# Attention and a ternary FFN on one core: first FFN weights made in two halves, query and key parts moved to GpSimd, and another written-out order

## The reference, cut to what matters

```python
xn = (x - mean) / sqrt(var + 1e-5)
# attention, 8 heads: queries and keys of 3 numbers a head, values of 16
scores = (q3 . k3) * scale + (q3 . dir_h) * (k3 . dir_h)     # causal
attn = softmax(scores) @ v ;  attn_out = attn @ Wo.T
# FFN, hidden size 512
def ternary(w): s = clip(mean(abs(w), axis=1), 1e-5); return clip(round(w / s), -1, 1), s
h = xn @ (t1 * s1).T + gate * (xn @ v.T @ fast_b.T @ u.T)
ffn_out = max(h, 0)**2 @ (t2 * s2).T
out = x + attn_out + ffn_out
```

## Time and profile before

| | before |
|---|---|
| median of 3 executions | 159.28 us (159.23 to 160.33) |
| profiled execution | 160.0 us, of which the span of its records is 158.3 us, and 1.7 us lie around it |
| granted clock of TensorE | 1.00 over the whole span |
| busy PE / DVE / ACT / POOL | 148.7 / 127.0 / 123.1 / 70.3 us |
| instructions | 3300 |
| zero matmuls | 47, the last at 52 us |

### The profile page before, as it was taken

How to read it: one execution, slowest core, us unless ns; L and a number is a source line. 1 busy time by engine, 2 the same in 40 slices (tenths; PEclk the granted TensorE clock), 3 DMA queues, 4 the chain that set the end, 5 groups by cost and what they waited for, 6 DMA issues and landing times.

```text
span 158.3 us, 3300 instructions
## 1 busy us (share of the span) xinstructions
PE 148.7 (94%) x1109; PEld 63.1 (40%) x1109; DVE 127.0 (80%) x423; ACT 123.1 (78%) x222; POOL 70.3 (44%) x126
## 2 busy tenths in 40 slices
PE   6999999999999999999999988898999989999992
PEld 2374446232242252232222222321736226885672
DVE  4688998999999999989999999999498885320442
ACT  0779795589588978898679999889899998878700
POOL 5038005942999689006931067013863225161520
PEclk9999999999999999999999999999999999999999
DMA  3760000240100170600000020000110200120202
GB/s 100 196 200 0 4 4 0 46 86 0 33 4 2 21 146 4 132 1 15 18 4 0 0 37 4 0 0 0 37 33 0 66 4 0 34 69 3 61 12 66
DMA packets 16621, 5.71 MB, mean 36 GB/s; under 512 B 11292, under 2 KB 16476, under 8 KB 16604
## 3 DMA queue, kind: packets, MB, share of 16 engines
q1 hardware_dynamic: 16208, 5.34, 14.8%
q10 hardware_dynamic: 396, 0.16, 0.4%
HBM read 1.96 MB, written 1.05 MB: 19 GB/s over the span
## 4 chain that ended last, share of the span: by engine, by line
PE 50%; ACT 32%; issue 7%; DVE 7%; POOL 1%; ACTq 1%; POOLq 0%; DVEq 0%
ACT Pr L757 21%; PE obank L973 8%; PE vbank L791 7%; PE vbank L922 6%; PE obank L798 6%; PE abank L950 5%; ACT abank L743 5%; PE abank L897 5%; PE abank L902 4%; DVE vbank L591 3%; PE abank L878 3%; ACT xn L663 2%; PE vbank L993 2%; DVE pm L588 2%; PE abank L849 1%
## 5 line engine op out<-in xcount | busy, mean ns | idle before, releaser
L757 ACT ACTIVATE Pr<-abank 128x1024 f32<-128x1024 f32 (+3 forms) x96 | 74.3, 817 | 7.9 <-PE abank L950 3.3
L591 DVE CUSTOM_DVE_ANT_0 vbank<-vbank,mask_row 128x128 f32<-128x128 f32 (+3 forms) x128 | 58.9, 524 | 4.4 <-PE vbank L922 3.9
L922 PE MATMUL vbank<-QK 32*128 32x512 bf16 (+3 forms) x192 | 40.4, 329 | 1.5 <-DVE xn L634 0.3
L588 DVE TENSOR_REDUCE pm<-vbank 128x1 f32<-128x512 f32 x64 | 39.5, 683 | 0.7 <-PE vbank L922 0.5
L973 PE MATMUL obank<-Pr,V 128*32 128x512 f32 (+3 forms) x384 | 39.2, 496 | 0.4 <-POOL Pr L454 0.4
L950 PE MATMUL abank<-QK 32*128 32x512 bf16 (+3 forms) x192 | 30.8, 331 | 2.1 <-ACT Pr L757 1.4
L454 POOL TENSOR_SCALAR_AFFINE_SELECT Pr<-Pr 128x512 f32<-128x512 f32 x32 | 20.1, 636 | 27.8 <-ACT Pr L757 27.6
L922 PEld LDWEIGHTS vbank<-QK 32*128 32x128 bf16 x192 | 11.5, 91 | 40.2 <-issue 17.4
L743 ACT ACTIVATE abank<-abank 128x256 f32<-128x256 f32 x64 | 23.3, 377 | 4.5 <-PE abank L950 3.7
L591 DVE DVE_READ_ACCUMULATOR2_ANT pm<- 128x1 f32 x128 | 18.4, 144 | 0.0
L798 PE MATMUL obank<-mask_row 128*128 128x512 bf16 x47 | 16.5, 447 | 1.3 <-POOL mask_row L386 1.3
(11 more groups left out here) (111 smaller groups left out, 129.5 us busy)
## 6 DMA issues: line engine op xcount, KB each, us to landing
x_sb<-in_L_attn_x SPq DMA_DIRECT2D x4, 256.0 KB, 3.5
out_y<-xn SPq DMA_DIRECT2D x8, 128.0 KB, 1.8
wfc_sb<-in_L_ffn_w_fc SPq DMA_DIRECT2D x1, 256.0 KB, 3.7
wpj_sb<-in_L_ffn_w_proj SPq DMA_DIRECT2D x1, 256.0 KB, 2.6
QK<-X SPq DMA_TRANSPOSE x10, 2.5
k_sb<-in_consts SPq DMA_DIRECT2D x1, 64.0 KB, 2.8
Wv_sb<-in_L_attn_Wv ACTq DMA_DIRECT2D x1, 64.0 KB, 3.4
Wo_sb<-in_L_attn_Wo ACTq DMA_DIRECT2D x1, 64.0 KB, 3.8
```

The lines of the kernel that those rows point to most:

```text
L588: last = nc.vector.tensor_reduce(out=least, in_=s_n, op=ALU.min, axis=AX.X)
L591: last = nc.vector.tensor_tensor_reduce(out=s_n, in0=s_n, in1=mask_row[:, CH - keys:CH], scale=1.0, scalar=3.0e38, op0=ALU.add, op1=ALU.mi ...
L757: nc.scalar.activation(Pr[:, n % PSLOTS, 2 * pair:2 * pair + 2, 0:cols], src[:, :, 0:cols], ACT.Exp, scale=-1.0).then_inc(free(unit), 1)
L922: last = nc.tensor.matmul(o[:, at:at + keys], QK[r, quarter(b, chunk), 0, g, q0:q0 + P], QK[r, quarter(b, half), 1, g, 0:keys], start=True ...
```

## The change

1. **First weights in halves.** "signs 0" makes four comparisons of 128x256 in place of two of 128x512 and counts each in `fc_signs`. "ternary 0" and the new "ternary 2" do half of the four GpSimd instructions each (128x256), counting `w1_ready` to 1 and 2. "w1" becomes "w1a" and "w1b", each with its low-rank product of 256 columns, two transposes, a bank of its own and its own copy by ACT. The first hidden-layer item of a quarter waits for w1a, the second for w1b.
2. **Query and key parts of quarters 1 to 3.** ACT now copies the numbers as float32 to SBUF instead of rounding them. GpSimd rounds, subtracts, rounds, subtracts (four instructions in place of two). DVE has no part in them, and ACT's copy of the values waits for no one.
3. **36 zero matmuls** in place of 47.
4. **Another order** of everything. In letters, the first hundred or so items:

```diff
@@ -126,7 +126,7 @@
-FILLERS = 47
+FILLERS = 36
...
@@ -150,7 +150,8 @@
         "W": [("mix", 0), ("weights", "wqk"), ("weights", "wvo")],
-        "F": [("signs", 0), ("ternary", 0)], "U": [("weights", k) for k in ("lora_u", "lora_b", "w1")],
+        "F": [("signs", 0), ("ternary", 0), ("ternary", 2)],
+        "U": [("weights", k) for k in ("lora_u", "lora_b", "w1a", "w1b")],
...
@@ -163,12 +164,12 @@
...
@@ -396,14 +397,20 @@
             wp = wpj_sb[:, :].rearrange("p (j c) -> p j c", j=HC)
-            ternaries = ((wfc_sb[:, :, :], fc_sc[:, 0, :, None].to_broadcast([P, HC, C]), fc_signs, w1_ready),
-                         (wp, pj_sc[:, 0:1, None].to_broadcast([P, HC, C]), pj_signs, w2_ready))
+            def hidden_half(n):
+                j = slice(n * HC // 2, (n + 1) * HC // 2)
+                return (wfc_sb[:, j, :], fc_sc[:, 0, j, None].to_broadcast([P, HC // 2, C]), tern[:, 0, :, j, :],
+                        fc_signs, 2 * (n + 1), w1_ready)
+            ternaries = (hidden_half(0), (wp, pj_sc[:, 0:1, None].to_broadcast([P, HC, C]), tern[:, 1, :, :, :],
+                                          pj_signs, 2, w2_ready), hidden_half(1))
...
                 if item[0] == "ternary":
-                    w, sc, signs, ready = ternaries[item[1]]
-                    pool.wait_ge(signs, 2)
-                    above, below = tern[:, item[1], 0, :, :], tern[:, item[1], 1, :, :]
+                    w, sc, marks, signs, count, ready = ternaries[item[1]]
+                    pool.wait_ge(signs, count)
+                    above, below = marks[:, 0, :, :], marks[:, 1, :, :]
...
@@ -411,7 +418,9 @@
                     q = item[1]
-                    pool.wait_ge(res_ready, q + 1)
+                    pool.wait_ge(hi_ready, q + 1)
+                    link(nc.gpsimd.tensor_copy(bf16_part(q, 0), rest(q)))
+                    link(nc.gpsimd.tensor_tensor(rest(q), rest(q), bf16_part(q, 0), ALU.subtract))
...
@@ -438,7 +447,7 @@
                     if c == 0:
-                        pool.wait_ge(w1_ready, 1)
+                        pool.wait_ge(w1_ready, 2)
...
@@ -535,14 +544,11 @@
                     nc.vector.tensor_copy(wall[:, C:VQK], filled(item)[:, 0:2 * NQ]).then_inc(free(item), 1)
-                elif kind == "qkv":
-                    q = item[1]
-                    src = qkv_view(item)[:, :, C:VQK].rearrange("p t (s c) -> p t s c", s=2 * G) if q else qk_rest()
-                    dve.wait_ge(hi_ready, q + 1)
-                    nc.vector.tensor_tensor(rest(q) if q else src, src, bf16_part(q, 0),
-                                            ALU.subtract).then_inc(res_ready, 1)
+                elif item == ("qkv", 0):
+                    dve.wait_ge(hi_ready, 1)
+                    nc.vector.tensor_tensor(qk_rest(), qk_rest(), bf16_part(0, 0), ALU.subtract).then_inc(res_ready, 1)
...
@@ -558,10 +564,12 @@
                         link(nc.vector.tensor_scalar(fc_sc[:, 2, :], fc_sc[:, 0, :], -0.5, None, ALU.mult))
-                        for k, op in enumerate((ALU.is_gt, ALU.is_lt)):
-                            nc.vector.tensor_tensor(tern[:, 0, k, :, :], wfc_sb[:, :, :],
-                                                    fc_sc[:, 1 + k, :, None].to_broadcast([P, HC, C]),
-                                                    op).then_inc(fc_signs, 1)
+                        for n in range(2):
+                            j = slice(n * HC // 2, (n + 1) * HC // 2)
+                            for k, op in enumerate((ALU.is_gt, ALU.is_lt)):
+                                nc.vector.tensor_tensor(tern[:, 0, k, j, :], wfc_sb[:, j, :],
+                                                        fc_sc[:, 1 + k, j, None].to_broadcast([P, HC // 2, C]),
+                                                        op).then_inc(fc_signs, 1)
...
@@ -692,7 +700,9 @@
                         src = qkv_view(item)[:, :, C:VQK].rearrange("p t (s c) -> p t s c", s=2 * G)
-                    nc.scalar.copy(bf16_part(q, 0), src).then_inc(hi_ready, 1)
+                    nc.scalar.copy(rest(q) if q else bf16_part(q, 0), src).then_inc(hi_ready, 1)
...
@@ -703,7 +713,6 @@
                     else:
-                        act.wait_ge(res_ready, q + 1)
...
@@ -766,8 +775,9 @@
                         ins = nc.scalar.activation(loraB, src[0:RANK, :], ACT.Copy, scale=gate_c[:, 0:1])
-                    elif item[1] == "w1":
-                        ins = nc.scalar.copy(w1T[:, :], src[:, :])
+                    elif item[1] in ("w1a", "w1b"):
+                        at = HID // 2 * (item[1] == "w1b")
+                        ins = nc.scalar.copy(w1T[:, at:at + HID // 2], src[:, 0:HID // 2])
...
@@ -820,14 +830,16 @@
                         last = nc.tensor.matmul(o[0:RANK, :], fb_sb[:, :], uT, start=True, stop=True)
-                    elif item[1] == "w1":
-                        pe.wait_ge(w1_ready, 1)
+                    elif item[1] in ("w1a", "w1b"):
+                        second = item[1] == "w1b"
+                        at = HID // 2 * second
+                        pe.wait_ge(w1_ready, 1 + second)
                         read(("weights", "lora_b"))
-                        nc.tensor.matmul(o[:, :], v_sb[:, :], loraB, start=True, stop=False)
-                        for j in range(HC):
-                            last = nc.tensor.matmul(o[:, j * P:(j + 1) * P], wfc_sb[:, j, :], ident,
-                                                    start=False, stop=j == HC - 1)
+                        nc.tensor.matmul(o[:, 0:HID // 2], v_sb[:, :], loraB[:, at:at + HID // 2], start=True, stop=False)
+                        for j in range(HC // 2):
+                            last = nc.tensor.matmul(o[:, j * P:(j + 1) * P], wfc_sb[:, HC // 2 * second + j, :], ident,
+                                                    start=False, stop=j == HC // 2 - 1)
...
@@ -892,7 +904,7 @@
                     o = empty(item)
-                    read(("weights", "w1"))
+                    read(("weights", "w1b" if j else "w1a"))
...
```

More of the change, by code:

```diff
@@ L165 @@
 WEAVE = """
-KKNNKKKKWKKKKKNKWNKCKXWFUQKKNKILVKNFUECKENNKKKKMMUNKMKNNMMHMMHMMXMJXQMMMVMQHMNILMVHRMMHMMHMMETKMMSIMAOMHMGMHMK
-MAMKMKMOAGOKDMGAMKMROKGKAMMHMOMMGHMMKXMAOMSJKMAGKKMTAOMKGKMDOALGMKMOAMKKGOKMGAMKKMKAODMGORKGMMDAPMAMOPMDSMGODA
-GOAOPPTPMMGGAQAMVMPDDMMAAMPMMAPMInAMPMAMPHAMHMJMMAAEMOOMMGLPMMGEAMMOAPMOGMARPMMGOAGADMOOPGGAMOMGTAMHMMSHMMDAnM
-PMAAMMPMADDMPAPPMMAMAPMASMAOMMnGOGPMMAOMRPGMAAOMMODTPGGAMOMMAPGAOGOMGMAAMMDPDMDAMAMPPMAMMASMPHAMHMMPAMMAMnPAMO
-MGPMOGMAPMMMADPYOGROGTSAOBAGOMAGOBGAYOMGAAMMDPMDMAPMADMPPABAMMMABAYASOMGAOMPMMAPGnOAMMPGMAROPGMMOMAGDAOPOYTDGP
-GAOAMMOGBMDADGPPOAGOBAGOBRTADGYBPnOGDAOAOGBYAGOAYOGBDBAGAOOPGPPABYGAOGDOAODGPPDGBYDAAPPOPOGGnDPPnBBYBYY
+KKKKKKNNKWNCKKKWKNFKKFKKXWUQKNIKKLKNNUEVUKNMNMHNMFMHUMMXEMMMQIMVNMLHMMMHMMXMHKRCHJMMMQMEMKVTMMAMOSMHGMMHMJKMMA
+RMOHGMAMNDOMHMMMKTGIJMAAOMMKOKMGKAGMMOLGKMAOKGXMDKMAOAMOGMKMAMGDOKDKMMAKMGKKMMAPOGMMROAGAOMPDMEOGGMAAOPOGMPMTM
+GPAQDDDVAMMnMPAMAMAMMIPAMMLAMPAMMAPMMHPMMOGAEOMHPMMGAPMOMAMMGODPAGMMOSGAOPMGRMATOMDDHGMMAOHMMMGAAMMPMAMMAPAMDM
+AMPnPPSAMMMAPAOMAMMOGPMMGAMPOAMGAMOSGORGDMPADMMOGMAPOAGOTMGAMMADMMAPMADMPnPMAMPSHMMSAHMnPAMAMMPMAOMMAGMPMMAMOG
+PMSOYAMGBSRAMOGODATDGOBMAGOGYDAOGPAMAMPMDAMPMMAPMABAMABAPMMYAOGPAOMGMAMOPMMAGPDAMOGRMPMAOGMOMADOGDnPTAMYGOABOG
+ABGOBAGMAODORTGGYBPAAOPPODBPGDGAAYOOBGGDAABPOOGAGDOPnYAGPPOBAGAOODPGDBYGnAOYAGPDOPGDPPPBBBnYYY
 """
```

## The result

| | before | changed |
|---|---|---|
| median | 159.72 us (159.23 to 160.33, 4 executions) | 162.57 us (162.1 to 164.36, 4 executions) |
| profiled execution | 160.0 us, span 158.3 | 162.43 us, span 160.7 |
| ratio | | 1.0197, 95% interval 1.0108 to 1.0286 |
| granted clock, mean | 1.00 | 0.987 |

Predicted were 158.1 us, 156.4 to 160.3. The changed kernel is slower by 2.9 us, outside the range and on the other side.

A forecast was written before the change was run, and what follows sets the result against it. Up to 110 us DVE's maxima set the pace, then PE and ACT are full. Terms of -0.5 - 0.3 - 0.8 + 0.7 - 0.3 = -1.2 us took the median from 159.28 to 158.1 us, range 156.4 to 160.3.

The forecast's parts named there:

- Part 4: Maxima between 15 and 36 us: PE's long items in the new order leave DVE gaps; +0.7 us, bounds -0.8 and +2.0.
- Part 3: Quarters 1 to 3: three subtractions leave DVE, GpSimd's waiting time hides its added work; -0.8 us.
- rival (c): Causal 2.4 and square 1 ahead of prep 3 on GpSimd start c = 3's scores 3.8 us later; 161.4, chance 0.13.
- signs of being wrong: Five zero matmuls at 0.44 each, DVE's gaps under 1 or over 3 us, or prep 3 over 1.5 us late.
- Part 1: Start: ten zero matmuls ahead of the query weights and five behind bring earlier transposes; -0.5 us, bounds -0.8 and +0.5.
- Part 2: Ahead of the first maxima: w1a and one zero matmul replace four zero matmuls; -0.3 us, bounds -0.6 and 0.
- rival (a): Between 15 and 110 us the maxima are fed nearly without gaps; 156.7 us, chance 0.27.
- part 5: w2 moves from c = 3, where DVE waited, to c = 2 in place of zero matmuls; -0.3 us, bounds -0.4 and 0.
- Part 6: Stage behind the maxima: same work and closing chain, order differs in details; 0, bounds -0.8 and +0.8 us.
- the other zero matmuls taken out: Zero matmuls removed elsewhere stood where PE waits for DVE anyway; no effect on the time.

The follow-up runs named there:

- e15: Changed kernel with the one-input form of the step ending every unit of maxima, and twelve and two zero matmuls at the start; 159.71 us, ratio 0.9979.
- e1: Changed kernel with the step ending units 2 to 5 of the maxima as a one-input reduction; 160.85 us, ratio 1.0011.
- e14: Changed kernel with twelve zero matmuls ahead of the query and key weights and two behind, held steps left; 164.37 us, ratio 1.0151.
- e4: Kernel before with square 3 ahead of prep 3 on GpSimd, started to run beside DVE's last step of c = 3; 161.22 us, ratio 1.0085.
- e13: Kernel before with the one-input form of the step ending every unit of maxima; 159.67 us, ratio 0.9998.
- e12: Kernel before with only the query and key parts of quarters 1 to 3 moved to GpSimd; 159.43 us, ratio 1.0.
- e2: Changed kernel with prep 3 ahead of square 1 on GpSimd; 166.69 us, ratio 1.0153.
- e5: e1 with five more zero matmuls: two ahead of the rows of group 0, two ahead of hidden item 0, one ahead of w1b; 161.44 us, ratio 1.0087.
- e6: e5 with the one-input form in all units and prep 6 ahead of causal 5.4 on GpSimd; 159.22 us, ratio 0.998.
- e11: Kernel before with ten zero matmuls ahead of the weights and five behind, in place of twelve and two; 159.26 us, ratio 0.998.
- e7: Kernel before without three of four zero matmuls ahead of the first maxima and two among those of c = 0; 159.47 us, ratio 0.9982.
- e10: e6 with twelve zero matmuls ahead of the query and key weights and two behind, in place of ten and five; 158.89 us, ratio 0.9958.
- e9: e6 with two zero matmuls instead of five between the query and key weights and the first transposes; 158.66 us, ratio 0.9954.
- e8: Changed kernel with the four score matmuls of one step in the held moment made four times; 163.48 us, ratio 1.0208.

## Why the prediction was wrong

**The step that failed** is the price of the new order. Part 4 calls itself "the price of the reordering", and it counts only the gaps that PE's long items leave. The same order moves GpSimd's work too, and the sum has no term for what that does to DVE. Part 3's "so nothing here" asked whether GpSimd had the time, and rival (c) whether prep 3 would be late; neither asked what DVE does in those moments. What the runs show in its place is the hold. Up to top 3 it cost 0.29 + 0.72 us (two copies, 0.46 and 0.89 for 0.17). At top 3 came 1.75 us for 0.18, worth 1.4 there and 1.1 more by the slower clock. Without the holds these two stretches are 0.9 us (first maxima to top 3, 55.85 and 54.97 in e15) and 2.6 us (top 3 to top 4) shorter. The one-input form alone brings it back (e1, e15 against e14), the hold put into the kernel before brings it about (e4), and the control is neutral (e13). The work that part 3 moved is not to blame, since alone it costs nothing (e12). The square that holds top 3 was in the prediction by name and place, in rival (c).

None of the prediction's signs of being wrong showed in the profile: the five zero matmuls took 0.25 each, DVE's gaps from the first maxima to 36 us are 1.3 us, and prep 3 started 0.07 us behind its maxima. They watched only what the sum had priced.

**Rival (c)** gave the right sign and almost the right number (161.4; measured 162.57) for a wrong reason, so its number is luck. Its condition was not met: the exponentials that causal 2.4 waits for ended before 71 (the mask started at 70.57), and prep 3 started at 73.16, 0.1 us behind square 1. What came of having the square there early is the hold. The range stopped short of (c), and the hold, which nobody had priced, lies beyond it.

**Part 1** (-0.5) came true in this profiled execution: transposes at 7.63 (foretold 7.65) and through at 8.35, 0.5 earlier; first maxima 0.55 earlier. But the moment at which 0.44 a zero matmul becomes 0.26 is not fixed, which the prediction had as a bound and not as a spread. Of the seven profiled kernels with ten and five in the new order, three (e2, e5, e6) had five at 0.46. Alone in the kernel before, part 1 is worth 0.2 us of 159.48, inside its interval (e11). The kernel before has that spread as well: its profile had the transposes at 7.83, e7's at 7.13, which is most of 160.0 against 158.97. So some of the 0.84 us at top 3 is the luck of the profiled start.

**Part 2** (-0.3) gave nothing: from the transposes' end to the first maxima it is 7.14 us (8.35 to 15.49) where it was 7.20. w1a took 1.33 us on PE (13.49 to 14.82) and not 1.0. With the zero matmul behind it PE is busy past the end of ACT's copy at 14.60, and the first score matmuls start 0.37 us behind that end, where it was 0.41. In the old order, with three zero matmuls simply gone, the same stretch did get 0.28 us shorter (e7).

**Part 3's gain** (-0.8) doesn't exist by itself (e12): a subtraction less on DVE becomes a wait for PE, in the kernel's old order. **Part 4** (+0.7) was mis-sized as well: with the holds gone, first maxima to top 3 take 54.97 us in e15 (15.73 to 70.70) and 56.14 in the kernel before, so parts 3, 4 and 5 together are -1.2, not -0.4. That lies between the forecast and rival (a), which had -2.0 for the three. DVE lacks 2.05 us from 15 to 36 in e15, 0.73 of it ahead of the first maxima: 1.3 is left among them, as much as before and not the 2.0 foretold. From 36 to 110 it lacks 1.51 us where it lacked 1.88, which is about part 5's -0.3.

**Part 6** (0, bounds 0.8): from top 3 to the end e15 takes 86.5 us, the kernel before 86.1, and e10 with prep 6 in its place 86.06. Inside its bounds. Prep 6 is a likely reason, but e10 has five zero matmuls more as well, and e6, with prep 6 in its place, takes 86.8.

**That the other zero matmuls taken out cost nothing** is true of the median (e7) and wrong for single executions. e1 has three of ten at 177 to 179 us and e15 three of twelve over 162, with a mean clock of 0.875 and 0.958 to 0.968. In the 32 executions of e5, e6, e9 and e10, which have five more behind the start, no mean clock is under 0.988. Which of PE's waits tips an execution over, and why e1 went so much further than e15, is open: no profiled execution of these two was a long one.

## What to carry to other kernels

When work moves to GpSimd or its order changes, list what VectorE runs in the same moments, and look at the short steps first: a step of 0.17 us that everything waits for was held here for nearly the whole of the GpSimd instruction beside it, 1.75 of 1.89 us. In a trace such a hold is no wait but an instruction that is up to ten times too long and ends with GpSimd's. The same step as a reduction with one input was not held, and cost nothing where there was no hold (e13). And read more than one execution of the start before an edit there is priced.

## What the runs showed of the hardware that was not expected

- A copy with one SBUF input (128x16 float32) is held like the two-input minimum, 0.89 for 0.17 us; a reduction over the same numbers isn't, 0.17 to 0.19 us beside the same GpSimd instructions (e1, e6, e15).
- One wait of PE of 0.89 us, with 1.11 us busy of 2, came ahead of a granted clock of 0.66 and 0.50 for about 4 us, worth 1.1 us. Behind a wait of 0.55 at the same place the clock stayed at 1.00 (e8). It isn't a matter of the wait alone: in e4 the clock fell in one execution of four.
- At the start zero matmuls of 512 columns take 0.44 to 0.46 us each in a row and later 0.25, 0.19 less, while the granted clock reads 1.00 in both places. It is probably the lower level of 1.2 GHz: in e2 a single one takes 0.39 us where the granted clock reads 1.00 (at 39.88) and 0.61 where it reads 0.50 (at 46.96), 0.22 more. When they reach 0.25 differs between executions by over 3 us, with the same ten at the start: in e8 before 5.1 (the ten took 3.75 us), in e5 not before 8.9.
